# The strict causal rule of head 0's scores: a product added in PSUM in place of a select on GpSimd

## What is computed

```
S = jax.nn.relu(att[:, 0])                 # head 0's scores, causal: key j <= query i
S = S.at[..., 0].set(0.0)                  # key 0 counts nothing
S = S * (1.0 - jnp.eye(T, dtype=S.dtype))  # nor does a token's own key: so strictly j < i
S_shifted = jnp.concatenate([jnp.zeros((B, 1, T), S.dtype), S[:, :-1]], axis=1)
FF = jnp.cumsum(S_shifted, axis=1)         # running sum over the queries
att = att - FF[:, None]                    # and the 101 least forgotten keys of a row are kept
```

## Time and profile before

| | us |
|---|---|
| median of three runs | 725.55 |
| the execution that was profiled | 726.16 |
| its span, first to last instruction | 724.4 |
| TensorE busy in it | 593.7 (82%) |
| VectorE busy | 547.0 (76%) |
| GpSimd busy | 442.3 (61%) |
| ScalarE busy | 382.7 (53%) |

### The profile page before, as it was taken

The page is one execution under the profiler, slowest core; times in us unless marked ns, Lnnn a source line. Parts: engine busy times, 40 slices in busy tenths (PEclk is TensorE's granted clock), DMA queues, the critical chain, the costliest instruction groups (busy, mean ns, idle before and its releaser), DMA issues. The chain is left out here.

```text
span 724.4 us, 16883 instructions
## 1 busy us (share of the span) xinstructions
PE 593.7 (82%) x5495; PEld 400.1 (55%) x5495; DVE 547.0 (76%) x2264; ACT 382.7 (53%) x813; POOL 442.3 (61%) x739
## 2 busy tenths in 40 slices
PE   4636798799978988799887888789887898789995
PEld 1414546466555655466565645566565665666573
DVE  7584957987698876987688866988579876987362
ACT  3552445655474555645474555645565555545452
POOL 6506656486846866486756856477655758357661
PEclk9956899989999999989999999989999999989998
DMA  4151630044001510034000510025000530000000
GB/s 91 15 58 16 69 35 1 16 56 49 2 16 22 67 17 1 16 51 55 1 16 20 62 24 1 17 39 63 3 1 2 64 40 1 2 13 5 1 1 16
DMA packets 27287, 18.99 MB, mean 26 GB/s; under 512 B 5417, under 2 KB 27072, under 8 KB 27200
## 3 DMA queue, kind: packets, MB, share of 16 engines
q1 hardware_dynamic: 27200, 17.91, 18.6%
HBM read 3.22 MB, written 2.10 MB: 7 GB/s over the span
## 5 line engine op out<-in xcount | busy, mean ns | idle before, releaser
L525 POOL TENSOR_SCALAR ar<-ar,mx 128x512 f32<-128x512 f32 (+3 forms) x512 | 286.2, 572 | 223.7 <-DVE mx L1227 223.2
L1227 DVE CUSTOM_DVE_ANT_0 ar<-ps_s,mask 128x512 f32<-128x512 f32 (+3 forms) x512 | 230.9, 483 | 28.5 <-PE ps_s L866 25.8
L879 PE MATMUL ps_t<-ident,ar 128*128 128x128 f32 x1280 | 211.0, 285 | 44.6 <-POOL ar L525 23.0
L692 ACT ACTIVATE pr<-ps_t 128x512 f32<-128x512 f32 (+1 forms) x352 | 190.3, 554 | 81.7 <-PE ps_t L879 79.7
L879 PEld LDWEIGHTS ps_t<-ident,ar 128*128 128x128 f32 x1280 | 158.5, 146 | 91.7 <-POOL ar L525 73.6
L866 PE MATMUL ps_s<-ks,qs 96*128 96x512 bf16 (+3 forms) x512 | 133.2, 313 | 19.9 <-DVE mx L1227 12.0
L898 PE MATMUL ps_o<-pr,va 128*32 128x128 f32 x2560 | 106.6, 299 | 8.4 <-ACT pr L692 7.2
L677 ACT ACTIVATE h<-ps_m,bi_col 128x512 f32<-128x512 f32 x64 | 44.0, 688 | 100.5 <-PE ps_m L813 100.5
L898 PEld LDWEIGHTS ps_o<-pr,va 128*32 128x32 f32 x2560 | 68.8, 118 | 41.7 <-ACT pr L692 19.8
L866 PEld LDWEIGHTS ps_s<-ks,qs 96*128 96x128 bf16 x512 | 42.9, 100 | 70.3 <-DVE mx L1227 34.3
L813 PE MATMUL ps_m<-zm,b_t 128*128 128x512 f32 x128 | 67.2, 606 | 5.2 <-ACT h L677 5.2
(11 more groups left out here) (215 smaller groups left out, 774.7 us busy)
## 6 DMA issues: line engine op xcount, KB each, us to landing
qs<-parts SPq DMA_DIRECT2D x48, 128.0 KB
ks<-parts SPq DMA_DIRECT2D x48, 128.0 KB
xs<-in_L_attn_x SPq DMA_DIRECT2D x8, 256.0 KB, 2.8
out<-res SPq DMA_DIRECT2D x8, 192.0 KB, 2.1
out<-res SPq DMA_DIRECT2D x8, 64.0 KB, 8.4
ar<-in_L_ffn_wi SPq DMA_DIRECT2D x1, 256.0 KB, 3.2
ar<-in_L_ffn_wo SPq DMA_DIRECT2D x1, 256.0 KB, 3.9
ar<-in_L_ffn_lora_B SPq DMA_DIRECT2D x4, 64.0 KB, 4.2
```

Source lines behind the costliest of these rows:

```text
L525: nc.gpsimd.tensor_scalar(col, col, -1.0, mx[:, t % NA_RING, j:j + 1], ALU.mult, ALU.add)\
L692: nc.scalar.activation(pr[:, u % NP_RING, 0:w], ps_t[u % NT_RING][:, 0:w], ACT.Exp, scale=-1.0)\
L879: last = nc.tensor.transpose(ps_t[u % NT_RING][:, P * j:P * j + P], ar[:, u % NA_RING, P * j:P * j + P], ident[:, :])
L1227: nc.vector.tensor_tensor_reduce(out=ar[:, t % NA_RING, w * j:w * j + w], in0=ps_s[t % NS_RING][:, w * j:w * j + w], in1=mask[:, k % 2, OF ...
```

## The change

The select of L496 and its semaphore are gone. A constant `later` in bf16 is built at the start, with zero where the query's number in the block is above the key's and -1e30 elsewhere. Behind each product of head 0's scores a second product, identity times `later`, adds this to the 128x128 diagonal block in PSUM, so that the ReLU makes zero of it. The scan now waits for ScalarE's read instead of the select. For image 0 TensorE also waits for `const` before the added product.

```diff
+        later = sb("later", [P, P], BF16)
...
+                    link(nc.gpsimd.memset(later[:, :], 0.0))
+                    link(nc.gpsimd.affine_select(out=later[:, :], in_=later[:, :], compare_op=ALU.is_gt, fill=-BIG,
+                                                 base=0, pattern=[[1, P]], channel_multiplier=-1))
...
-                            if t == at(f"s{a}", n):
-
-                                wait_read(pool, f"s{a}", n)
-                                edge = s0[:, FOFF[a]:FOFF[a] + P]
-                                nc.gpsimd.affine_select(out=edge, in_=edge, compare_op=ALU.is_gt, fill=0.0, base=0,
-                                                        pattern=[[1, P]], channel_multiplier=-1).then_inc(ruled, 1)
...
-                                last = nc.tensor.matmul(m[:, 0:T - P * j], head0[1][:, P * j:P * j + P],
-                                                        head0[0][:, P * j:T], start=True, stop=True)
+                                nc.tensor.matmul(m[:, 0:T - P * j], head0[1][:, P * j:P * j + P],
+                                                 head0[0][:, P * j:T], start=True, stop=False)
...
-                                last = nc.tensor.matmul(m[:, 0:T - P * j], ks[:, c, 0, P * j:P * j + P],
-                                                        qs[:, c, 0, P * j:T], start=True, stop=True)
+                                nc.tensor.matmul(m[:, 0:T - P * j], ks[:, c, 0, P * j:P * j + P],
+                                                 qs[:, c, 0, P * j:T], start=True, stop=False)
+                            if n == 0:
+                                pe.wait_ge(const, 2)
+                            last = nc.tensor.matmul(m[:, 0:P], ident16[:, :], later[:, :], start=False, stop=True)
...
-                        dve.wait_ge(ruled, NA * n + j + 1)
+                        wait_read(dve, f"s{j}", n)
```

More of the change, by code:

```diff
@@ L311, in build @@
                  "summed", "taken", "m_full", "act_read", "dve_read", "varred", "rooted", "xn_done",
-                 "limited", "ruled", "centred", "split", "stacked", "less_done", "exp_done",
+                 "limited", "centred", "split", "stacked", "less_done", "exp_done",
                  "hot_wide", "scanned", "nf_done", "cut_set", "counted", "rested", "parted", "again",
@@ L328, in build @@
         b_ready = s["b_ready"]
-        again, limited, ruled, centred = s["again"], s["limited"], s["ruled"], s["centred"]
+        again, limited, centred = s["again"], s["limited"], s["centred"]
         x_d = x.rearrange("b (a p) c -> b p a c", p=P)
```

## The result

The changed kernel takes 732.45 us (732.11 to 735.77, four executions) against 726.21 (724.4 to 727.91, four) for the kernel before: a ratio of 1.0097, interval 1.0057 to 1.0136. That is 6.2 us, where 1.6 were forecast and 731.0 was the upper end of the range. It is slower by more than the 0.5% that can be told from no change. So there are two questions: what the change costs by itself, and what made the first comparison larger.

The account below looks back on a forecast made before the run. TensorE was taken to bound the kernel; 0.8 us steady, 0.5 start and 0.3 hand-over made 1.6 us, giving 727.2 us against the median of 725.55 (727.8 against the profiled execution). The range was 723.0 to 731.0.

Parts of the forecast that it names:

- What bounds the kernel: Steady passes: TensorE waits for no GpSimd shift or scan, so time VectorE gains becomes its idle time.
- The removal at nothing: Scans of columns 1 and 2: 32 selects with their waits go, 0.79 us a pass for VectorE, worth nothing overall.
- Rival 1: VectorE sets the pace and its 5.5 us of select waits come back whole: 721.7 us, chance 0.14.
- Steady part, 0.8 us: Seven steady passes on TensorE: products of `s0` and `s2` exposed, `s1` and `s3` hidden, 0.11 us a pass.
- The start, 0.5 us: Image 0 on gapless TensorE: all four products exposed at 0.1 us each plus some load loss; upper bound 1.2 us.
- The order of scan and `hsum`: Steady pass: column 1's scan goes before GpSimd's `hsum`, taking 0.95 us instead of 1.94; `hsum` grows to about 2.2.
- hand-over, 0.3 us: Slot 17's shift to TensorE's `turn`: it just fits, with 0.04 us a pass added for the signal.
- Rival 2: Slot 17's shift lands late for the `turn`, about 0.5 us lost each pass: 730.7 us, chance 0.10.
- GpSimd's constants at nothing: Start: an added memset and select, about 0.7 us, hidden in GpSimd's 1.52 us idle before the norm's root.
- Rival 3: Products do not stream; each of the 32 costs its full 0.219 us, 7.0 us in all: 732.6 us, chance 0.06.
- the sum's last step: Whole kernel: 0.8 + 0.5 + 0.3 = 1.6 us taken as the total, nothing added for effects elsewhere.
- The last sentence of the prediction: Stages outside these slots where VectorE or GpSimd sets the pace: answering to the shifted order would prove it wrong; no size.

Follow-up runs that it names:

- e_removal2: Kernel before with the selects gone, no products added, and the flag that starts the repeated search multiplied by zero: 724.41 us, 0.9992.
- bare pair: Both kernels with one row instead of eight in images 2 to 7's stack transfers, plus extra products ahead of slots 36 to 38's turns: 711.79 and 714.19 us.
- e_double: Changed kernel with each added product standing twice: 727.88 us, ratio 1.0045 to the kernel before.
- e_products: Kernel before with the products added and the selects and their waits kept: 729.81 us, 1.0068.
- e_select0: Changed kernel with the select kept in image 0 and products only for images 1 to 7: 727.2 us, 1.0036.
- e_keep_after: Changed kernel with nine extra products of 512 columns for each of images 0 to 6, where TensorE otherwise waits: 716.83 us, 0.9905.
- e_fill8: Kernel before with eight more identity products in TensorE's idle time behind the first transposes: 725.28 us, 1.0005.
- e_keep_before: Kernel before with nine extra products of 512 columns for each of images 0 to 6, where TensorE otherwise waits: 712.73 us, 0.9839.
- three pairs with one or both disturbances cut: Both kernels with stack transfers cut, with TensorE kept busy by extra products, or with both: differences 2.36, 4.1 and 2.40 us.
- e_after: Changed kernel measured again without any edit: 727.63 us against 725.84 for the kernel before, 1.0038.

## Why the prediction was wrong, step by step

- **What bounds the kernel: right.** TensorE does. VectorE's gain became idle time (0.82 to 2.18 us ahead of `nf`), and e_removal2 gives 0.9992.
- **The removal at nothing: right,** by e_removal2. Rival 1 is refuted.
- **Steady part, 0.8 us: right.** `s0` and `s2` exposed, `s1` and `s3` hidden in waits that shrank by 0.06 each; 0.11 a pass in the bare pair, over the six passes of images 2 to 7.
- **The start, 0.5 us: the mis-sized term.** It measured 1.62 at the matmul behind the score products and 1.25 at the first mask step, both above the bound of 1.2. I costed the short product by a row in which it stands beside others of its kind, and took the float32 pairs around it to cost what they did before. They became up to 0.30 us longer; their loads, 0.50 us a pair, are the likely reason.
- **The order of scan and `hsum`: right,** with 0.95 for the scan. The three shifts behind it were in time for the `turn`, so the **hand-over, 0.3 us,** measured 0. Rival 2 is refuted.
- **GpSimd's constants at nothing: nothing speaks against it.** The start's shift is accounted for by TensorE's rows.
- **Rival 3: refuted,** by e_double and by every 0.06 in the timelines.

With the terms as measured the sum is 0.8 + 1.6 + 0 = 2.4 us, or 2.0 with what of the start reaches the first mask step. Against the median shown 2.4 would have been 728.0, inside the range and inside "within 0.5%".

Two steps failed: the start's 0.5 us, by 0.8 to 1.1 us, and above it the sum's last step, that nothing outside the slots of the change adds to it. It put TensorE's clock and its pauses at nothing without a reason. The last sentence of the prediction named an effect outside the slots, but looked for it where VectorE or GpSimd sets the pace; it came in TensorE's own stream. In the first profiled pair, 6.0 us apart at the last mask step, 2.0 is the change as summed, about 1.8 the pauses (2.55 at the first place less 0.8 at the second), and the rest, about 2.2, lies in the slots where the clock stretches differ.

How far this belongs to the change differs between the two. The longer clock stretches stand in every profiled execution of the changed kernel. The pauses do not favour either side: of the eight profiled executions with products and full transfers six pause (the changed kernel in all four comparisons, e_products, e_double; not e_select0 and e_keep_after), of the four without products all four (before, e_fill8 and e_removal2 at the second place, e_keep_before at both). A pause behind 927 matmuls stands in six of the eight and one of the four, one at the second place in five of the eight and all four. The standstill is 2.5 us for an execution on average with the products and 2.2 without. In two of the three later sets of the changed kernel, and in that of e_keep_before, the profiled execution is the slowest of all; how often the executions without a profile pause can't be seen.

The later comparisons gave 1.8, 1.9 and 5.0 us, e_products 4.0, and the three pairs with one or both disturbances cut 2.4, 4.1 and 2.4. All lie on the slower side; whether the change costs the 2.0 to 2.4 of its slots or a us or two more, these runs can't settle.

**What stays open.** Why all four executions of the first comparison lie at 732.1 or above, when only 2 of the 36 later ones do. Pauses alone don't make it: the profiled execution holds 2.77 us of them and is the fastest of the four. The pace in the start moves executions too, by about 2 us between two of the same kernel (1.97 us, above), but the other three weren't profiled. And why the packet ahead of matmul 927 comes late in the changed kernel. It starts at 162.6 us in before and in e_fill8, and at 171.9, 170.3 and 172.2 in after, e_products and e_after, though the packet before it starts between 150.8 and 153.4 in all five.

The Trainium skill, page "Runtime: NRT & Kernel Launch", section "Instruction fetch mechanics", says that instructions come in blocks of 16 KiB, 256 of them, over a queue of the engine's own, and that crossing a block is mostly hidden. The two places are 2050 matmuls apart, 4100 instructions with their loads, close to 16 such blocks; by this the cost would be about nothing, and the traces show up to 2.82 us.

## What to carry to other kernels

- An added matmul costs its start-to-start time, 0.06 us here and not the recorded 0.22. But look at its neighbours and their loads as well: between pairs of float32 matmuls the same product cost up to 0.51 us, and four in the start cost twice what 28 in the steady passes did.
- Relieving an engine pays only where another waits for it. Here 5.5 us of VectorE's waiting went and the time stayed.
- Where a change of 2 us is forecast in a kernel whose executions scatter over 8 or 10, leave room for events outside the edit's slots; and look for TensorE's idle slots at the lower clock first. Filling them was worth 11.4 us, against 2 to 5 for everything this change does.
- A wait that the profile puts down to an engine is worth a second look: see when that engine's instruction ended. Here it had ended 2.4 us before, and a pause of the kernel before was taken for a wait.

## What the runs showed of the hardware that I had not expected

- TensorE can stand still for 0.6 to 2.8 us with all inputs at hand, always behind 927 or about 2977 recorded matmuls in this program, also in kernels without the change: in ten of the twelve profiled executions with full stack transfers and in none of the four with the transfers cut. All 16 pauses end 1.50 to 1.82 us after a 16 KB packet of the instruction queue has landed.
- In the start matmuls went at one of two paces: the score products of columns 1 to 3 took 2.76 us in the earlier trace rows and 1.46 in e_select0. The column of the granted clock doesn't show it: from 16 to 26 us it is 1.00 in the kernel before (20 matmuls in 10 us) and 0.66 in e_select0 (33 matmuls), whose first 3 us of this stretch went at the fuller pace. There the durations are to be believed. The row of e_select0, busy us and counts as in the earlier trace rows:

```profile
16.00:26.00 10.00, 9.97 (x33) 6.08 (x33) 6.54 (x28) 5.78 (x15) 5.48 (x9) 0.66 0.00 1
```

- Nine products of 512 columns for each image, work that is thrown away, made the kernel before faster by 1.6% (0.9839 [0.9817, 0.9861]).
